# Cross attention in eight steps per tile: four 32-row score matmuls side by side, one exponential over two banks

## What is computed

```python
q = rope(Wq @ layernorm(x) + bq)      # 8 heads of 8 channels; the first 4 channels of a head are turned
k = rope(Wk @ c + bk)
v = Wv @ c + bv
p = softmax(q @ k.T / sqrt(8))        # 256 x 256 for each head of each batch
x = x + tanh(g) * (Wo @ (p @ v) + bo)
```

## Time and profile before

| | |
|---|---|
| device time, median of 3 runs | 1577.44 us (1573.41 to 1581.14) |
| the profiled execution | 1564.62 us, its span 1562.6 us |
| PE, DVE, ACT, POOL busy | 93%, 61%, 50%, 34% of the span |
| attention | from 0 to 586 us of the span |
| the 32 maxima turned on PE (one a tile) | from 42.7 to 561.9 us |

### The profile page before, as it was taken

One profiled execution on the slowest core, in us unless ns is written; L12 is line 12 of the kernel. 1 busy time (PEld: TensorE's weight loads), 2 busy tenths in 40 slices (PEclk: granted clock), 3 DMA queues, 4 the chain that ended last, 5 costly groups with the idle time before them and its releaser, 6 DMA issues. The chain is left out here.

```text
span 1562.6 us, 32056 instructions
## 1 busy us (share of the span) xinstructions
PE 1451.1 (93%) x10096; PEld 1209.4 (77%) x10097; DVE 953.7 (61%) x1817; ACT 775.4 (50%) x1425; POOL 535.0 (34%) x592
## 2 busy tenths in 40 slices
PE   3999999999999986999988999999978699999998
PEld 2777777777777755888877888888867478888887
DVE  7888887888788734776655433333324466666653
ACT  4466666666666663333223333333332656666652
POOL 4332332332333201744455443320005344455220
PEclk9999999999999995999999999999995799999999
DMA  5122122112212202211265332221125001111000
GB/s 176 57 57 62 53 55 62 54 53 62 55 52 62 54 3 77 105 41 55 71 196 190 121 94 91 91 67 54 50 57 175 27 28 41 42 42 41 15 14 28
DMA packets 89081, 106.54 MB, mean 68 GB/s; under 512 B 12208, under 2 KB 80432, under 8 KB 88368
## 3 DMA queue, kind: packets, MB, share of 16 engines
q1 hardware_dynamic: 79264, 73.60, 15.9%
q0 software_dynamic: 9744, 31.99, 6.4%
HBM read 54.29 MB, written 25.03 MB: 51 GB/s over the span
## 5 line engine op out<-in xcount | busy, mean ns | idle before, releaser
L422 ACT ACTIVATE e_t<-st_ps 128x512 f32<-128x512 f32 x512 | 277.9, 595 | 165.7 <-PE st_ps L527 165.2
L369 DVE TENSOR_REDUCE row_max<-s_ps 128x4 f32<-128x1024 f32 x256 | 311.0, 1217 | 32.5 <-PE s_ps L510 32.4
L510 PE MATMUL s_ps<-k_st,q_st 96*128 96x256 f32 x1024 | 196.7, 315 | 13.0 <-DMA q_st<-q_part 11.7
L527 PE MATMUL st_ps<-q_st,k_st 104*128 104x256 f32 x1024 | 170.2, 287 | 1.6 <-ACT e_t L422 1.5
L510 PEld LDWEIGHTS s_ps<-k_st,q_st 96*128 96x128 f32 x1024 | 147.4, 193 | 21.9 <-DMA q_st<-q_part 12.5
L527 PEld LDWEIGHTS st_ps<-q_st,k_st 104*128 104x128 f32 x1024 | 143.6, 189 | 6.6 <-ACT e_t L422 5.2
L546 PE MATMUL o_ps<-e_t,v_st 128*32 128x256 f32 x2048 | 137.0, 385 | 0.9 <-ACT e_t L422 0.9
L1599 POOL DMA_INDIRECT gathered_tail<-sorted_results,result_at x64 | 70.1, 1095 | 153.7 <-POOLq L2090 135.4
L1457 PE MATMUL y_ps_moe<-w_all_moe,xt_hi_moe 128*128 x568 | 113.3, 283 | 3.8 <-DVE xt_lo_moe L1276 3.8
L1836 DVE TENSOR_TENSOR h_all_tail<-silu_tail,u_ps_tail 128x512 f32<-128x512 f32 x64 | 43.9, 685 | 115.5 <-ACT silu_tail L1707 65.1
L1282 DVE TENSOR_TENSOR h_all_moe<-silu_moe,u_ps_moe 128x512 f32<-128x512 f32 x71 | 48.8, 687 | 107.2 <-PE u_ps_moe L1435 107.2
(11 more groups left out here) (310 smaller groups left out, 3592.6 us busy)
## 6 DMA issues: line engine op xcount, KB each, us to landing
k_st<-k_part SPq DMA_DIRECT2D x384, 32.0 KB
q_st<-q_part SPq DMA_DIRECT2D x96, 128.0 KB, 3.2
stage_moe<-in_experts POOLq DMA_DIRECT2D x21, 512.0 KB, 4.3
rows_in_moe<-sorted_rows SPq DMA_DIRECT2D x71, 128.0 KB, 2.0
sorted_results<-y_sb_moe SPq DMA_DIRECT2D x71, 128.0 KB
c_in<-in_ctx SPq DMA_DIRECT2D x33, 128.0 KB, 2.1
xn_moe<-in_ctx SPq DMA_DIRECT2D x8, 512.0 KB
context_tail<-in_ctx SPq DMA_DIRECT2D x8, 512.0 KB, 10.9
```

The source lines that it names most:

```text
L369: nc.vector.tensor_reduce(out, s_ps[s_ // 2 % 2][:].rearrange("p (j h) t -> p j h t", j=2), AX_X, ALU.max).then_inc(s["max_taken"], 1)
L422: nc.scalar.activation(e_t[h % 8][:], st_ps[h % 2][:], ACT.Exp, scale=float(DH) ** -0.5)\
L510: last = nc.tensor.matmul(s_ps[s_ // 2 % 2][:, 2 * (h - s_) + half_, :], q_st[r][0:ROWS, u, half_ * P:(half_ + 1) * P], k_st[r][0:ROWS, u, ...
L527: last = nc.tensor.matmul(st_ps[h % 2][:, half_, :], k_st[r][0:MROWS, u, j, half_ * P:(half_ + 1) * P], q_st[r][0:MROWS, u, :], start=True ...
```

## The change

A body now has eight steps `p`, two heads each, and the stacked operands are laid out anew: every head has its own 32 partitions with its three products, two rows of maxima and zeros, so that a score matmul contracts over 32 rows, and four of them lie in four different groups of rows. In a step PE issues two plain and two turned score matmuls for one half of the columns and then for the other. The turned scores have one buffer of two banks instead of two of one bank, and ACT takes one exponential over both. Values are issued by halves of a unit, in every step. `k_st` is a quarter of its size. The biases of q and k are turned once at the start (`turned_bias`) and added by POOL in an instruction of its own (`bare`, then `whole`); DVE's multiplication is one instruction instead of two. The bias of v goes into the output bias; the copy of v moves from DVE to ACT. Layernorm's subtraction and multiplication move from DVE to POOL and one body earlier. `y_sb` is made in step 5 instead of step 0 of the body; POOL's addition of it still stands between k's parts and q's parts. SP sends three k and three q DMAs of 128 KB a tile, instead of twelve of 32 KB and three of 128 KB, and one DMA of zeros to the rows of maxima.

```diff
-    LAG = 8
-    ROWS, MROWS = 96, 104
+    STEPS = HP // 2
+    LAG = 5
+    MAX_ROWS = slice(3, P, 16)
...
-        k_st = [sb(f"k_st{r}", [P, UNITS, UH, D], F32R) for r in range(RING)]
+        k_st = [sb(f"k_st{r}", [P, UNITS, D], F32R) for r in range(RING)]
-        e_t = [sb(f"e_t{r}", [P, 2, D]) for r in range(8)]
+        e_t = [sb(f"e_t{r}", [P, 2, 2, D]) for r in range(4)]
-        st_ps = [ps(f"st_ps{r}", [P, 2, D]) for r in range(2)]
+        st_ps = ps("st_ps", [P, 2, 2, D])
...
+        def later(p, lag):
+            return (p - lag) // STEPS, (p - lag) % STEPS
...
+                    sp.wait_ge(s["k_high"], n + 3)
+                    for t in range(2):
+                        sp.dma_start(k_st[r][t:P:4, :, :].bitcast(F32), part["k"][:, 0, :].bitcast(F32))\
+                            .then_inc(k_stacked[r], 16)
...
+                    sp.wait_ge(s["q_high"], n + 3)
+                    for t in (0, 2):
+                        sp.dma_start(q_st[r][t:P:4, :, :].bitcast(F32), part["q"][:, 0, :].bitcast(F32))\
+                            .then_inc(q_stacked[r], 16)
                     sp.wait_ge(s["q_split"], n + 3)
+                    sp.dma_start(q_st[r][1:P:4, :, :].bitcast(F32), part["q"][:, 1, :].bitcast(F32))\
+                        .then_inc(q_stacked[r], 16)
...
                 if there(n, c, 2):
+                    parts_of("k", n, c, i)
                 if there(n, c, -2):
                     pool.wait_ge(s["y_taken"], n - 1)
+                    row = x_row(n - 2)
+                    nc.gpsimd.tensor_tensor(row, row, like_row(n, y_sb), ALU.add).then_inc(s["y_free"], 1)
+                if there(n, c, 2):
+                    parts_of("q", n, c, i)
+                if there(n, c, 3):
+                    normalize(n, 3)
...
+                nc.gpsimd.tensor_tensor(bare[a][:], roped[a][:, 0, :], roped[a][:, 1, :], ALU.add)\
+                    .then_inc(s[a + "_summed"], 1)
+                pool.wait_ge(s[a + "_summed"], n + 3)
+                nc.gpsimd.tensor_tensor(whole[a][:], bare[a][:], turned_bias[a][:], ALU.add).then_inc(s[a + "_whole"], 1)
...
+                for p in range(STEPS):
+                    k, t = later(p, LAG)
+                    if there(n, c, k):
+                        g = STEPS * (n + k) + t
+                        act.wait_ge(s["st_scored"], g + 1)
+                        nc.scalar.activation(e_t[t % 4][:], st_ps[:], ACT.Exp, scale=float(DH) ** -0.5)\
+                            .then_inc(s["exp_done"], 1)
...
+                    if p == 5 and there(n, c, -2):
                         act.wait_ge(s["y_projected"], n - 1)
                         act.wait_ge(s["y_free"], n - 1)
                         nc.scalar.activation(y_sb[:], misc[:, 0:D], ACT.Identity, bias=out_bias[:],
                                              scale=tanh_gain[:, 0:1]).then_inc(s["y_taken"], 1)
...
+            def score_step(n, c, i, p):
+                k, t = later(p, LAG)
+                turned = list(scores_turned(c, k, t)) if there(n, c, k) else []
+                plain = list(scores(c, p)) if there(n, c, 1) else []
+                if turned:
+                    if t == 0:
+                        pe.wait_ge(m_stacked[(c + k) % RING], 16 * uses(c, i, k))
+                    wait_count(pe, s["exp_done"], STEPS * (n + k) + t)
+                    wait_alone(pe)
+                if plain:
+                    if p == 0:
+                        pe.wait_ge(q_stacked[(c + 1) % RING], 64 * uses(c, i, 1))
+                        pe.wait_ge(k_stacked[(c + 1) % RING], 48 * uses(c, i, 1))
+                    wait_count(pe, s["max_taken"], (n + 1) * STEPS + p - 1)
+                for at in range(0, 4, 2):
+                    for of, done in ((turned, "st_scored"), (plain, "scored")):
+                        for out, w, moving in of[at:at + 2]:
+                            last = nc.tensor.matmul(out, w, moving, start=True, stop=True)
+                        if of and at == 2:
+                            last.then_inc(s[done], 1)
```

More of the change, by code:

```diff
@@ L223, in body @@
-                    sp.wait_ge(s["q_split"], n + 3)
[L224 to L229, removed]
+                    sp.dma_start(k_st[r][2:P:4, :, :].bitcast(F32), part["k"][:, 1, :].bitcast(F32))\
+                        .then_inc(k_stacked[r], 16)
@@ L241, in body @@
+            normalize(0, 0)
+            for r in range(1, RING):
+                nc.gpsimd.memset(q_st[r][:].bitcast(F32), 0.0).then_inc(s["q_cleared"], 1)
+            pool.wait_ge(s["bias_summed"], 2)
             def body(n, c, i):
                 if there(n, c, 2):
[L243 to L247, removed]
@@ L254, in body @@
[L254 to L267, removed]
-                        nc.gpsimd.tensor_copy(part[a][:, 0, :], whole[a][:]).then_inc(s[a + "_high"], 1)
-                        pool.wait_ge(s[a + "_high"], n + 3)
-                        nc.gpsimd.tensor_tensor(part[a][:, 1, :], whole[a][:], part[a][:, 0, :].bitcast(F32),
-                                                ALU.subtract).then_inc(s[a + "_split"], 1)
@@ new lines, in turn_out @@
+            def turn_out(b):
+                for half_, u in ((h, u) for h in range(2) for u in range(2)):
+                    at = (2 * half_ + u) * P
+                    last = nc.tensor.transpose(misc[:, at:at + P], o_sb[b][:, u, half_ * P:(half_ + 1) * P],
+                                               ident[:])
+                last.then_inc(s["o_turned"], 1)
+            def body(n, c, i):
+                for p in range(STEPS):
+                    score_step(n, c, i, p)
+                    use_values(n, c, p)
+                    if p == 0 and there(n, c, 2):
+                        if there(n, c, -2):
+                            pe.wait_ge(s["o_normed"], 2 * (n - 1))
+                        else:
@@ new lines, in body @@
+                    if p == 4 and there(n, c, -1):
+                        if there(n, c, -2):
+                            pe.wait_ge(s["a_taken"], n - 1)
+                        else:
+                            pe.wait_ge(s["q_roped"], n + 3)
+                        pe.wait_ge(s["o_taken"], 2 * (n - 1) + 1)
+                        turn_out(0)
+                    if p == 5 and there(n, c, -2):
+                        pe.wait_ge(s["a_taken"], n - 1)
+                        if there(n, c, -1):
+                            pe.wait_ge(s["o_normed"], 2 * (n - 1) + 1)
+                        nc.tensor.matmul(misc[:, 0:D], w_out[:], a_t[:], start=True, stop=True)\
+                            .then_inc(s["y_projected"], 1)
@@ L470, in body @@
+                    if p == 6 and there(n, c, 2):
+                        if there(n, c, -2):
+                            pe.wait_ge(s["y_taken"], n - 1)
+                        elif there(n, c, -1):
+                            pe.wait_ge(s["o_normed"], 2 * (n - 1) + 1)
+                        else:
+                            pe.wait_ge(s["q_roped"], n + 3)
                         for h in range(2):
@@ L552, in _, with value_bias @@
-            steps(pe, body)
+                        pe.wait_ge(s["o_normed"], 2 * (n - 1) + 1)
+                        pe.wait_ge(s["o_taken"], 2 * n)
+                        turn_out(1)
+            def value_bias():
+                pe.wait_ge(more_consts_in, 3 * 16)
+                pe.wait_ge(s["v_stored"], 1)
+                nc.tensor.matmul(misc[:, 0:1], w_out[:], bias[:, 5:6], start=True, stop=True)\
+                    .then_inc(s["value_bias_made"], 1)
+            steps(pe, body, None, value_bias)
```

457 lines of the change are left out of this document (214 added, 243 removed).

## The result

The changed kernel takes 1685.88 us, the median of 4 runs (1682.43 to 1689.71). The kernel before, timed beside it, takes 1575.43 us (1572.04 to 1581.14). The ratio is 1.070, with a 95% interval of 1.066 to 1.074. The forecast was 1667 us in a range from 1605 to 1780.

A forecast was written before the change was run, and what follows sets the result against it. PE (TensorE) was taken to set the 16.75 us period. 28 periods of 20.2 us and three of 14.5 made 90 us more: 1564.6 to 1655, plus 12.8 for the median, 1667 us; range 1605 to 1780.

The forecast's parts named there:

- The wait that is last: q's parts stand behind POOL's y addition; PE idles 4.7 us a tile, period 18.85 us at full clock.
- rival (c): Faster: q copies land in 2.0 us, clock stays, a step needs 1.5 us; 1545 us, chance 0.12.
- Terms of the chain: Within a body: `y_sb` at 11.37 us, q's low part at 15.15, third q copy landed at 18.8.
- PE's share of a step: Eight score matmuls in four overlapping row groups take 0.45 us; PE needs about 13.3 us a tile.
- Rival (b): The four row groups do not overlap, weight loads stay in a row; 1739 to 1778 us, chance 0.15.
- The loop through the exponential: Scores, exponential, next scores through one buffer: at least 1.66 us a step, about 14.5 us a tile.
- The clock: PE's idle time in each tile halves its clock; step 0 gets 1.4 us longer, period 20.2 us.
- Rival (a): The same wait for q, but PE's clock is kept: period 18.85 us, 1629 us, chance 0.20.
- The end of the attention: After the last turn of the maxima: the same chain of exponentials, unchanged within 5 us.
- The start: Before the first turn of the maxima: waits for the same loads, unchanged within 5 us.
- The sum: Between first and last turn of the maxima: 609 us against 519.2, 90 us more; median 1667 us.

The follow-up runs named there:

- e1: The changed kernel with POOL's addition of y moved behind q's parts, nothing else: 1518.05 us, ratio 0.969 to the kernel before.
- e4: The changed kernel with both POOL's addition of y behind q's parts and PE's two waits exchanged: 1483.28 us, ratio 0.947 to the kernel before.
- e2: The changed kernel, stall kept, with six unread filler matmuls on PE at the end of each body: 1619.93 us, ratio 1.034 to the kernel before.
- e3: The changed kernel with the maxima's wait on the empty instruction and the exponential's on the matmul: 1661.02 us, ratio 1.060 to the kernel before.
- e8: The changed kernel with four more unread plain-score matmuls a step in the last bodies; only the tail was read: 26.5 us instead of 35.0.
- e5: e4 with both column halves of a head's scores issued one after the other: 1497.4 us, ratio 0.949 to the kernel before.

## Why the prediction was right, step by step

**The wait that is last: right, and this decided the case.** q is made behind the addition of y, y comes out of step 5, and PE stands still at the next body for the third q DMA. e1 took that one order away and the kernel became 3.1% faster than before. Without this wait the result would have been on the side of rival (c), faster, and lower than its 1545 us.

**Terms of the chain.** `y_sb` comes at 11.83 us with a full clock, not 11.37. The missing term is the empty instruction, below: without it in front, in e4, it comes at 11.32. The part that POOL does behind it was met within 0.01 us (3.79 against 3.78). From q's low part to PE it is 2.7 to 2.8 us instead of 3.65: the third copy lands about 2.35 us after its issue (328.10 to 330.45), where I took 3.2 from the earlier trace rows. Rival (c) had argued for this one term with the twelve small k copies that no longer surround it; no run here varied them, so the reason stays argued. The prediction also leaned on 4.9 us at the start of the trace, in which it said that PE was idle. That was misread: PE still did plain scores in it and was idle for 2.21 us before 38.75, as the bracket in the earlier trace rows says; the 4.9 us are only the way from the low part to the scores. The errors of opposite sign, +0.5 and -0.9, leave the warm period at 18.37 us in e2 against 18.85, and with the clock term, 0.6 too low, the period of the kernel is 20.38 against 20.2. That it fits so closely is in part luck: three errors cancel.

**PE's share of a step: right.** The eight scores take one wave of four after another. The distance from the first score to the first value matmul is 0.44 us at full clock, in e4 (308.46 to 308.90), against 0.45. Rival (b) is out. In the weight loads shown under e4 the eight of a step are through in 0.30 us (308.46 to 308.76); in a row, at the 0.112 us of the earlier trace rows, they would need 0.9. The Trainium skill gives two rules here (page "TensorE: Matmul & The Clock Gate"): its section "LDWEIGHTS (loading the stationary operand)" prices a load by its columns alone, its Part 3 has a load overlap with matmuls in flight where the row groups differ. The trace bears out both: one load over 32 rows takes 0.18 us, as one over 96 does in the kernel before (0.19), but the second four start at 308.57, while the matmuls of the first four (0.38 us from 308.46) still run.

**The loop through the exponential: the mechanism right, one term missed.** I counted 0.06 us from the end of an exponential to PE's next load, from the earlier trace rows. It is 0.23 in the changed kernel, since the wait now stands on an empty instruction ahead of the matmul. The diff shows that instruction (`wait_alone`), and I gave it no price. e4 measured it: 1.1 us a tile when nothing else stalls. In the changed kernel the swap left the period as it was (20.46 against 20.38 in e3): the steps got shorter, but the half clock lasted 7.7 us a tile instead of 6.7. The unstalled period was forecast at 14.5 us and came out at 15.12 with the empty instruction in front and 14.02 without.

**The clock: right in kind, low by 0.6 us.** 2.0 us per tile instead of 1.4 (e2). The half clock lasts 6.7 us a tile, not 3 to 4. I took its length from the one stall at the start of the trace, and counted step 0 alone. Against e2 step 0 is 1.55 us longer, step 1 0.30 and step 2 0.21. Rival (a), the clock kept, is out.

**The end of the attention: wrong.** I took it as unchanged within 5 us. It is 10.9 us longer: the last bodies run at half clock, though PE has work all the time. The same stretch of the changed kernel and, below it, of the kernel before:

```profile
656.00:686.00 30.00, 27.52 (x172) 11.86 (x168) 1.85 (x7) 15.36 (x19) 1.45 (x2) 0.54 0.01 2
```

```profile
562.00:582.00 20.00, 16.68 (x157) 10.12 (x156) 1.65 (x6) 14.32 (x29) 0.74 (x1) 1.00 0.01 3
```

I had looked at the chain of exponentials there, which at full clock is indeed within the 5 us (26.5 us in e8 against 24.1), but not at whether the clock would stay up; the other 8.5 of the 10.9 us are the half clock. The start was right: 3.1 us earlier.

**The sum.** Forecast for the turns of the maxima 90 us more, measured 96.2: 569.6 for the 28 bodies that add a y and make a q, 20.34 each (565.6 forecast), and 45.8 for the other three (43.5). With the tail, less the start, that is 104 us more from the change itself. So the terms above are 14 us too low (6 tiles, 8 tail and start). The unchanged code adds another 14 in the profiled execution, which the forecast does not have. Against that, the forecast took the median 12.8 us above the profiled execution, and it lies 3.5 above it. Together that is the 19 us by which the median exceeds the forecast.

## What to carry to other kernels

When a producer is moved later in a loop, list everything that stands behind its consumer in that engine's program order. Here one addition of 0.73 us on an engine that was idle nearly two thirds of the time held back q and turned a gain of 3% into a loss of 7%, and moving it by one place gave that back. Where one instruction can carry one wait, put the wait that comes last on the working instruction and the early ones on the empty instruction (here 0.17 us a step). Price a short stall of TensorE with the clock that it costs: here 3.5 us of idle time brought 2.0 us on top, and a stretch that loses half of its side-by-side matmuls can lose the clock too.

## What the runs showed of the hardware that was not expected

**Matmuls of different groups of rows start out of the order of issue.** In e5 two turned matmuls of one group are issued first, then two plain ones of another; in the records a plain one starts 0.01 us behind the first turned one and ahead of every other turned one. If each wave has one matmul of each group, what was issued second starts 0.2 us later. The Trainium skill, page "TensorE: Matmul & The Clock Gate", Part 3, describes matmuls as strictly in order; these records differ from that, and the measured result decides. In time it made next to nothing, 0.13 us a tile.

**Busy by the records is not the same as a full clock.** In the tail of the changed kernel PE is busy 27.52 of 30 us at a granted clock of 0.54, at the end of the kernel before 16.68 of 20 at 1.00. Four more matmuls a step, in the other two groups of rows, brought 0.96 to 1.00 in each of the four versions where they were tried; e3 had 0.99 without them.

**Going from the values to the full array stops the weight loads for 0.41 us at full clock.** So it is before the output turns and projections that follow values ("[0.41 <-issue]" in the loads of e4), the same 0.41 as in the earlier trace rows. It is not the price of every change of the array's split: from the scores to the values the loads of e4 stand for 0.14 us (308.76 to 308.90). The Trainium skill, page "TensorEngine Tiling (Array Packing)", section "Key Properties", says that changing the tiling drains TensorE; the trace agrees, with a different stop for each kind of change.
